# Non-local block, 16 images on one core: theta and phi of both halves gathered in one bank, theta's stack filled by transfers

## The reference

```python
theta = jnp.einsum('bhwc,cd->bhwd', x, W_theta)             # 256 -> 32 channels
phi = _maxpool2x2(jnp.einsum('bhwc,cd->bhwd', x, W_phi))    # 256 -> 32
g = _maxpool2x2(jnp.einsum('bhwc,cd->bhwd', x, W_g))        # 256 -> 128
beta = jax.nn.softmax(jnp.einsum('bqd,bkd->bqk', theta, phi), axis=-1)
tmp = jnp.einsum('bqk,bkv->bqv', beta, g).reshape(B, H, W, Cc // 2)
o = jnp.einsum('bhwv,vc->bhwc', tmp, W_o)
return gamma * o + x
```

## Time and profile before

| | |
|---|---|
| median of two runs | 240.32 us (240.01 and 240.63) |
| span of the profiled execution | 237.7 us; no time of its own is listed beside it |
| TensorE busy | 232.0 us, 98% |
| VectorE, GpSimd, ScalarE busy | 205.3, 167.3, 147.8 us |
| moved by DMA | 51.14 MB, mean 215 GB/s |

### The profile page before, as it was taken

The page is one execution under the profiler, slowest core; times in us unless marked ns, Lnnn a source line. Parts: engine busy times, 40 slices in busy tenths (PEclk is TensorE's granted clock), DMA queues, the critical chain, the costliest instruction groups (busy, mean ns, idle before and its releaser), DMA issues.

```text
span 237.7 us, 4361 instructions
## 1 busy us (share of the span) xinstructions
PE 232.0 (98%) x1464; PEld 207.8 (87%) x1464; DVE 205.3 (86%) x475; ACT 147.8 (62%) x274; POOL 167.3 (70%) x119
## 2 busy tenths in 40 slices
PE   7999999999999999999999999999999999999994
PEld 4777888988989899898989989898998989989794
DVE  5699988989888898988989899898988989899785
ACT  3665948577483866838477492847748385645640
POOL 1488698868679686768867677786867868642870
PEclk9999999999999999999999999999999999999999
DMA  7693029396592937739194683928659293725854
GB/s 238 220 365 128 3 70 337 130 272 258 119 374 88 337 151 242 292 105 382 60 327 191 194 341 108 343 85 289 241 150 383 61 338 139 247 107 190 318 204 181
DMA packets 14934, 51.14 MB, mean 215 GB/s; under 512 B 1856, under 2 KB 2496, under 8 KB 14912
## 3 DMA queue, kind: packets, MB, share of 16 engines
q1 hardware_dynamic: 14512, 50.67, 60.6%
q10 hardware_dynamic: 400, 0.20, 0.3%
HBM read 33.95 MB, written 16.78 MB: 213 GB/s over the span
## 4 chain that ended last, share of the span: by engine, by line
PE 89%; DMA 5%; DVE 4%; issue 1%; ACT 1%; SPq 0%; DVEq 0%
PE proj L209 23%; PE out L350 18%; PE proj L216 12%; PE proj L350 8%; PE score L255 6%; PE shift L350 6%; PE shift L310 5%; PE score L350 4%; PE score L282 4%; DMA x_t<-in_xt 2%; DMA out<-y_sb 2%; PE shift L209 1%; DVE y_sb L669 1%; DVE neg_parts L643 1%; PE score L265 1%; PE out L282 1%
## 5 line engine op out<-in xcount | busy, mean ns | idle before, releaser
L564 POOL TENSOR_TENSOR e_lo<-e_sb,e_hi 128x512 fp32r<-128x512 f32 x64 | 82.0, 1294 | 45.7 <-ACT e_sb L488 45.7
L559 POOL TENSOR_TENSOR x_lo<-x_t,x_hi 128x1024 fp32r<-128x1024 f32 x30 | 71.8, 2399 | 8.7 <-ACT x_hi L444 8.7
L485 ACT ACTIVATE e_hi<-shift 128x512 fp32r<-128x512 f32 x60 | 36.0, 600 | 17.9 <-PE shift L310 17.0
L209 PE MATMUL proj<-x_hi,w_hi 128*128 128x512 f32 x118 | 46.8, 397 | 0.1
L209 PE MATMUL proj<-x_hi,w_lo 128*128 128x512 f32 x118 | 46.6, 395 | 0.0
L643 DVE TENSOR_REDUCE neg_parts<-score 128x2 f32<-128x512 f32 x64 | 43.6, 686 | 1.1 <-PE score L255 0.2
L350 PE MATMUL out<-G_lo,e_hi 128*128 128x258 f32 x132 | 37.4, 284 | 0.0
L350 PE MATMUL out<-G_hi,e_hi 128*128 128x258 f32 x132 | 37.4, 283 | 0.0
L216 PE MATMUL proj<-x_lo,w_hi 128*128 128x512 f32 x118 | 37.3, 396 | 0.0
L350 PE MATMUL out<-G_hi,e_lo 128*128 128x258 f32 x132 | 37.2, 282 | 0.0
L488 ACT ACTIVATE e_sb<-shift 128x512 f32<-128x512 f32 x60 | 36.1, 602 | 0.0
(11 more groups left out here) (107 smaller groups left out, 480.8 us busy)
## 6 DMA issues: line engine op xcount, KB each, us to landing
x_t<-in_xt SPq DMA_DIRECT2D x32, 512.0 KB, 5.2
x_n<-in_xn SPq DMA_DIRECT2D x32, 512.0 KB, 7.6
out<-y_sb SPq DMA_DIRECT2D x31, 512.0 KB, 6.2
w_sb<-in_w_proj SPq DMA_DIRECT2D x1, 256.0 KB, 2.8
theta<-neg_hi ACTq DMA_DIRECT2D x16, 4.0 KB
theta<-neg_lo SPq DMA_DIRECT2D x16, 4.0 KB
out<-y_sb SPq DMA_DIRECT2D x1, 256.0 KB, 2.1
wo_sb<-in_w_out SPq DMA_DIRECT2D x1, 128.5 KB, 5.7
```

What stands on the lines that cost most here:

```text
L209: nc.tensor.matmul(bank_[:, :], w[:, c, cols:cols + P], x_hi[:, i % 2, h, c, :], start=(c == 0 and n == 0), stop=False)
L485: nc.scalar.activation(e_hi[:, i % 2, n, :], shift_bank(i, n)[:, :], ACT.Exp)
L559: nc.gpsimd.tensor_tensor(x_lo[:, i % 2, h], x_t[:, i % 2, h], x_hi[:, i % 2, h].bitcast(f32), ALU.subtract).then_inc(x_lo_ready, 1)
L564: nc.gpsimd.tensor_tensor(e_lo[:, i % 2, n, :], e_sb[:, n, :], e_hi[:, i % 2, n, :].bitcast(f32), ALU.subtract).then_inc(e_lo_ready, 1)
```

## The change

`theta_phi(i)` now projects both halves into one bank, 12 matmuls in one accumulation. The weights lie in SBUF as 64 zero columns, 64 columns of W_theta and W_phi, 64 zero columns, then W_g. For half 0 the matmul takes the block's columns and the zeros after it, for half 1 the zeros before it and the block. So the bank has theta and phi of half 0 on partitions 0 to 63 and of half 1 on 64 to 127. It is a bank of its own, proj[1] (proj[0] for image 1), until values(i, 1) takes it.

From there `theta_high` is one cast of 128 x 512 for an image, `phi_pool` one pool and `theta_low` one subtraction, in this order by their waits. They write theta_hi and theta_lo, not the stack. `theta_into_stack`, on SyncE's queue, copies theta's 32 rows of each half into the stack by six transfers inside SBUF and phi's second copy by a seventh; scores wait for these. x_t has three buffers in place of two. The start is rewritten, and in a step scores(b, 0) comes first, then theta_phi(a).

```diff
+        theta_hi, theta_lo = sb("theta_hi", [P, HALF], f32r), sb("theta_lo", [P, HALF], f32r)
...
-        phi_max = outb[1][THETA:P, 0:NK]
+        phi_max = outb[1][:, 0:P]
...
+        def tp_bank(i):
+            return proj[0] if i == 1 else proj[1]
...
+            def theta_into_stack(i):
+                sp.wait_ge(theta_hi_ready, i + 1)
+                for h in range(2):
+                    rows, pixels = slice(TP * h, TP * h + DK), slice(HALF * h, HALF * (h + 1))
+                    for r in (0, 2 * DK):
+                        sp.dma_start(theta[r:r + DK, i % 3, pixels].bitcast(f32),
+                                     theta_hi[rows, :].bitcast(f32)).then_inc(theta_in, 16)
+                sp.wait_ge(phi_hi_ready, 2 * i + 2)
+                sp.dma_start(phi[DK:2 * DK, i % 3, :].bitcast(f32),
+                             phi[0:DK, i % 3, :].bitcast(f32)).then_inc(phi_in[i % 2], 16)
+                sp.wait_ge(theta_lo_ready, i + 1)
+                for h in range(2):
+                    rows, pixels = slice(TP * h, TP * h + DK), slice(HALF * h, HALF * (h + 1))
+                    sp.dma_start(theta[DK:2 * DK, i % 3, pixels].bitcast(f32),
+                                 theta_lo[rows, :].bitcast(f32)).then_inc(theta_in, 16)
...
             for s in range(2, LAST):
                 a, b, d = s, s - 1, s - 2
+                theta_into_stack(a)
                 max_into_stack(b)
...
+            def theta_phi(i):
+                if i == 0:
+                    pe.wait_ge(fixed_ready, 8)
+                    pe.wait_ge(w_lo_ready, 2)
+                    pe.wait_ge(x_hi_ready, 1)
+                    pe.wait_ge(x0_lo_ready, 2 * CC)
+                else:
+                    pe.wait_ge(x_hi_ready, 2 * i + 1)
+                    pe.wait_ge(x_lo_ready, 2 * i + 2)
...
+                for h in range(2):
+                    cols = slice(TP * (1 - h), TP * (3 - h))
+                    for c in range(CC):
+                        for n, (w, x) in enumerate(((w_hi, x_hi), (w_lo, x_hi), (w_hi, x_lo))):
+                            last = nc.tensor.matmul(tp_bank(i)[:, :], w[:, c, cols], x[:, i % 2, h, c, :],
...
             def values(i, h):
                 if i == 1:
                     pe.wait_ge(g_pooled, h + 1)
                 elif i > 1:
-                    pe.wait_ge(theta_lo_ready, 2 * i + h + 1)
-                    pe.wait_ge(phi_pooled, 2 * i + h + 1)
-                project(i, h, P, value_bank(i, h), g_ready)
+                    pe.wait_ge(theta_lo_ready, i + h)
+                    pe.wait_ge(phi_pooled, i + h)
...
             def scores(i, n):
                 if n == 0:
-                    pe.wait_ge(theta_lo_ready, 2 * i + 2)
+                    pe.wait_ge(theta_in, theta_loads(i))
+                    pe.wait_ge(phi_in[i % 2], loads(i))
...
-            first_project()
-            values(0, 0)
-            theta_phi(0, 1)
+            first_values()
+            theta_phi(0)
             values(0, 1)
-
-            theta_phi(1, 0)
+            theta_phi(1)
+            values(1, 0)
             scores(0, 0)
             scores(0, 1)
-            values(1, 0)
+            values(1, 1)
             scores(0, 2)
             scores(0, 3)
-            theta_phi(1, 1)
             turn_max(0)
-            values(1, 1)
             mix(0)
 
-            theta_phi(2, 0)
             scores(1, 0)
-            theta_phi(2, 1)
+            theta_phi(2)
             shifted(0, 0)
             shifted(0, 1)
...
-            def theta_high(i, h):
-                act.wait_ge(tp_ready, 2 * i + h + 1)
-                nc.scalar.copy(theta[0:THETA, i % 3, HALF * h:HALF * (h + 1)],
-                               proj[h][0:THETA, :]).then_inc(theta_hi_ready, 1)
+            def theta_high(i):
+                act.wait_ge(tp_ready, i + 1)
+                if i > 0:
+                    act.wait_ge(theta_in, theta_loads(i - 1))
+                nc.scalar.copy(theta_hi[:, :], tp_bank(i)[:, :]).then_inc(theta_hi_ready, 1)
...
+            def phi_pool(i):
+                dve.wait_ge(theta_hi_ready, i + 1)
...
+                v.tensor_reduce(phi_max, tp_bank(i)[:, :].rearrange("p (w n) -> p n w", w=WIN),
                                 AX.X, ALU.max).then_inc(phi_pooled, 1)
...
+            def theta_low(i):
+                v.tensor_tensor(theta_lo[:, :], tp_bank(i)[:, :], theta_hi[:, :].bitcast(f32),
                                 ALU.subtract).then_inc(theta_lo_ready, 1)
```

More of the change, by code:

```diff
@@ L19 @@
 GW = C + 2
-PROJ = P + DV
+TP = 2 * DK
+PROJ = TP + DV
+WG = 3 * TP
 WARM = 8
@@ L91, in nonlocal_block @@
         x0_in = sem("x0_in")
-        xt_in = [[sem(f"xt_in{s}{h}") for h in range(2)] for s in range(2)]
+        xt_in = [[sem(f"xt_in{s}{h}") for h in range(2)] for s in range(3)]
         xn_in = [[sem(f"xn_in{s}{h}") for h in range(2)] for s in range(2)]
@@ L118, in loads_t, with theta_loads @@
         def loads_t(i, h):
-            return loads(i) - 16 if i % 2 == 0 and h == 0 else loads(i)
+            return 16 * (i // 3) if i % 3 == 0 and h == 0 else 16 * (i // 3 + 1)
+        def theta_loads(i):
+            return 6 * 16 * (i + 1)
         def neg_loads(i):
@@ L153, in _ @@
             sp.dma_start(wo_sb[:, :], w_out).then_inc(wo_in, 16)
-            for i in (1, 2):
-                for h in range(2):
-                    load_t(i, h)
+            for h in range(2):
+                load_t(1, h)
+            theta_into_stack(0)
+            for h in range(2):
+                load_t(2, h)
             for h in range(2):
                 load_n(0, h)
+            theta_into_stack(1)
             for h in range(2):
@@ L201, in first_project @@
                     w, x = ((w_hi, x_hi), (w_lo, x_hi), (w_hi, x_lo))[n]
-                    last = nc.tensor.matmul(proj[0][:, :], w[:, c, 0:P], x[:, 0, 0, c, :],
+                    last = nc.tensor.matmul(value_bank(0, 0)[:, :], w[:, c, WG:], x[:, 0, 0, c, :],
                                             start=(n == 0 and c == 0), stop=(n == 2 and c == 0))
[L204 to L227, removed]
+                last.then_inc(g_ready, 1)
             def values(i, h):
@@ L395, in _ @@
                 if s > 2:
-                    for h in range(2):
-                        theta_phi(a, h)
-                        scores(b, h)
-                        shifted(d, 2 + h)
-                    for h in range(2):
-                        values(a, h)
-                        scores(b, 2 + h)
+                    scores(b, 0)
+                    theta_phi(a)
+                    shifted(d, 2)
+                    values(a, 0)
+                    scores(b, 1)
+                    shifted(d, 3)
+                    values(a, 1)
+                    scores(b, 2)
+                    scores(b, 3)
                 if a < LAST:
@@ L519, in _ @@
                 if s > 2:
-                    for h in range(2):
-                        theta_high(a, h)
-                        exps(d, 2 + h)
+                    theta_high(a)
+                    exps(d, 2)
                     phi_high(a)
+                    exps(d, 3)
                 if a == 2:
@@ L732, in _ @@
                 if s > 2:
-                    for h in range(2):
-                        phi_pool(a, h)
-                        theta_low(a, h)
-                        maxima(b, h)
+                    maxima(b, 0)
+                    phi_pool(a)
+                    theta_low(a)
+                    maxima(b, 1)
+                    g_pool(a, 0)
                     phi_low(a)
-                    g_pool(a, 0)
                     maxima(b, 2)
```

130 lines of the change are left out of this document (74 added, 56 removed).

## The result

The changed kernel takes 260.57 us (median of 259.75 and 261.40), the kernel before 240.32: ratio 1.0846, 95% interval 1.0757 to 1.0934. It is slower, by 20.3 us where 15.2 were predicted, and the median lies 0.6 us above the range. The profiled execution took 261.40 us, with a span of 259.6, so 21.9 more than the span before.

A forecast was written before the change was run, and what follows sets the result against it. TensorE was taken as the bound, its own work unchanged. Start order 10.9, clock 1.9, steps 2.1 and image 15 0.3 sum to 15.2 us on 240.3, so 255.5 us; range 250 to 260.

The forecast's parts named there:

- Value nought: In the steps: 1.4 us of VectorE work saved per step of 14.09 us gains nothing, since TensorE hides it all.
- The walk of the start: At the start: the new order of the queues makes TensorE wait before theta_phi(0), (1) and (2), costing about 10.9 us.
- The clock's term: In the start's gaps: TensorE's clock falls to half rate once, costing 1.9 us; bounds none or three falls (5.7 us).
- I count one fall: At the gap before theta_phi(1), 4.1 us: one fall to half rate, 1.9 us, all paid; given 42%.
- The rival built on it: At the start: the clock falls in three gaps, 259.3 us; two or three falls together were given 25%.
- The step's term: In 13 steps: values(a,1) waits for theta_low(a), 0.16 us each, 2.1 us in all.
- The other waits have room: In the steps: waits besides values(a,1) cost nothing; GpSimd's queue ends at 13.3, 1.0 us before theta_phi asks.
- Image 15's 0.3 us: In the last image's step: its scores come in the same step as its transfers, adding 0.3 us (0 to 0.8).
- The rival of late transfers: In 13 steps: the transfers land late and scores(b,0) waits some 0.3 us each, 4 us, 259.5 us; given 5%.
- That of the zero columns: In theta and phi's 192 matmuls: zero columns allow shorter spacing, 21.9 us saved, 233.6 us; 8% with a misjudged start.

The follow-up runs named there:

- the kernel with every mend: Changed kernel with both step waits mended, start reordered, warm-up matmuls in start gaps and the end mended, last version redo_fill_tail2; steps 14.12 us, 245.92 us.
- d_fill_gaps: Changed kernel plus 32 warm-up matmuls with zeros in the start's idle gaps, order otherwise unchanged; 259.11 us, ratio 1.0783 to the kernel before.
- a_xhigh_first: Changed kernel with x_high(1,1) moved ahead of theta_high(0) in ScalarE's start list; 258.47 us, ratio 1.0746 to the kernel before.
- b_xlow_early: Changed kernel with x_low(a+1,0) ahead of e_low(d,2) on GpSimd and its x_high ahead of theta_high(a) on ScalarE; 259.36 us, steps 14.27.
- redo_fill_tail2: Changed kernel with both step edits, start reordered, warm-up matmuls in start gaps, end mended, maxima(0,0) ahead of VectorE's g_pool(1,*); 245.92 us, ratio 1.0253.
- before_transfers3: Kernel before plus seven spare SBUF transfers per image that nothing reads, for images 3 to 15 only; 240.27 us, ratio 1.0005.
- c_scores_first: Changed kernel with scores(b,2) ahead of values(a,1) on TensorE; 261.47 us, ratio 1.0900 to the kernel before, steps 14.48.
- bc_both_waits: Changed kernel with the edits of b_xlow_early and c_scores_first together; 259.44 us, ratio 1.0842 to the kernel before, steps 14.11.

## Why the prediction was right in kind and 5 us short

- "Value nought" for what ScalarE and VectorE save was right. VectorE gives up 20.9 us, and the kernel with every mend has the steps of the kernel before, 14.12, not shorter ones. TensorE has the same 1464 matmuls in both, and in the steps only its list and its waits count.
- The walk of the start was right in size: 10.9 us predicted, about 11.2 by d_fill_gaps. Its first gap ended at 10.27 for 9.95. The 2.0 us by which theta_phi(1) came later than 18.45, and the further 1.9 of theta_phi(2), are 1.7 and 1.5 us of half rate in the block of twelve ahead of it, and little else. One wait was misplaced: TensorE stood before scores(0,3), for the maxima, and not before theta_phi(2); x_low(2,1) ended at 34.56, and theta_phi(2) started at 35.07, behind mix(0) at half rate. shifted(0,0) came at 39.17, for 34 to 36.
- The clock's term was mis-sized: "I count one fall", 1.9 us; there were three stretches of half rate on the chain, worth about 4.7. That is the step that failed first. I had counted falls by the idle time ahead of one row at the end, and taken only the gap longer than that. But the clock also fell behind 2.51 us of idle time before scores(0,3), and the half rate in which the start began lasted through the gap before theta_phi(0). The rule that I quoted of the Trainium skill, page "TensorE: Matmul & The Clock Gate", Part 1, speaks for a fall in every long gap. Here the trace agrees for both gaps that TensorE entered at full rate, and a_xhigh_first's for the first gap too (2.82 us). The rival built on it, 259.3 us, had the clock right, within 1.0 us; that it lies only 1.3 us under the measured time is in part luck, since it missed the step's second wait and most of the end.
- The step's term was half of it: 2.1 us predicted, 4.4 measured. Its mechanism and its size hold: values(a,1) waits 0.17 us in 13 steps. What failed is the sentence "The other waits have room". It sets the end of GpSimd's queue against theta_phi alone. By its own durations g_low(a) ends 10.9 us after a step's start (6.5 + 1.29 + 2.40 + 0.73), and mix(a) asks at 10.9 too (135.34 against scores(b,0) at 124.43); that pair I never compared. b_xlow_early shows it at 0.21 us a step, 2.5 in twelve.
- Image 15's 0.3 us was 0.7 for scores(15,0). With the waits of step 15 ahead of it (0.4 us) and shifted(15,0) behind it (0.3, for its row of maxima) the end is 1.6 us longer.
- Put together: order 11.2, clock 4.7, steps 4.4 and end 1.6 are the 21.9 us between the two spans; predicted were 10.9, 1.9, 2.1 and 0.3. The medians lie 20.3 us apart.
- The rival of late transfers, 259.5 us, came nearest in number and had the mechanism wrong: the scores wait for them in step 15 alone. That of the zero columns fell by a spacing of 0.24 us.

Still open: of the 4.6 us that turn_max(1) remains behind in redo_fill_tail2, its trace names 0.6 us for theta's transfers, 1.7 filled ahead of shifted(0,0) for the maxima's row, and 0.8 in three short waits. Its first matmuls also stand 0.43 us apart, until 10.0 us, where those of before stand 0.23 apart; how much of that another wait would have covered is not shown. Whether another order wins these was not tried.

## What to carry to other kernels

When TensorE is the bound, its gaps can cost twice: once as idle time, and once as the half rate that followed the long ones here, so price every gap of a predicted timeline with both, not the longest alone. When you move an instruction, compare its end with each of its readers; two waits in series hide one another, and mending the nearer one alone shows nothing. Transfers that are free in the steps can be dear at the start, by what stands behind them in the queue that issues them.

## What was not expected of the hardware

The clock's column can read 1.00 where the matmuls stand 0.43 us apart: so in the changed kernel from 5.66 to 13.8 us, with these stretches:

```profile
5.00:10.00 5.00, 3.00 (x7) 1.00 0.80 302
10.00:15.00 5.00, 4.73 (x13) 1.00 0.01 5
```

And whether the start begins at half rate changes from one execution to the next, with the same code: in the profile of before the matmuls from 5.47 us on stand 0.23 us apart, in that of before_transfers3, which has the same start, 0.43 until 9.6. There TensorE was kept busy and the rate recovered; in the changed kernel, with the gap before theta_phi(0), it lasted to 13.8. In a_xhigh_first and c_scores_first the first values stand 0.23 us apart, and the half rate came only behind that gap, until 14.8 and 15.9 us. So in a_xhigh_first:

```profile
6.39 0.39 PE L257 MATMUL shift<-x_hi,w_hi 128*128 128x512 f32 x1
6.62 0.40 PE L257 MATMUL shift<-x_hi,w_lo 128*128 128x512 f32 x1
...
10.31 0.47 PE L242 MATMUL proj<-x_hi,w_hi 128*128 128x512 f32 x1 [2.82 <-DVE x_lo L743]
...
11.84 0.63 PE L242 MATMUL proj<-x_hi,w_hi 128*128 128x512 f32 x1
12.27 0.63 PE L242 MATMUL proj<-x_hi,w_lo 128*128 128x512 f32 x1
```

Nor does the length of a gap alone settle it: behind scores(15,0)'s wait of 1.7 us in d_fill_gaps the clock fell, behind its 2.0 us in bc_both_waits it did not (granted clock 1.00 from 228 us on).

The four executions of d_fill_gaps lie 3.2 us apart, the seven of before beside them 1.4.
